# Attention weights turned by a transposing DMA: one row tile of each head leaves TensorE, and every engine's order is laid out anew

## The reference, cut to what matters

```python
for i in range(NUM_BLOCKS):                       # 4
    y = _cond_layer_norm(x, cond, s1_w[i], s1_b[i], b1_w[i], b1_b[i])
    y = _sparse_attention(y, src, dst, wq[i], bq[i], wk[i], bk[i], wv[i], bv[i], wo[i], bo[i])
    x = x + y
    y = _cond_layer_norm(x, cond, s2_w[i], s2_b[i], b2_w[i], b2_b[i])
    y = jax.nn.relu(y @ m_w1[i] + m_b1[i]) @ m_w2[i] + m_b2[i]
    x = x + y
```

## Time and profile before

| | |
|---|---|
| time, three runs | 1119.53 us median (1119.4 to 1120.54) |
| span of the profiled execution, first to last instruction | 1117.2 us; its own time is not listed apart |
| PE busy | 1066.1 us (95%) |
| DVE, ACT, POOL busy | 773.4, 577.6, 673.3 us |
| mean granted TensorE clock | 0.992 of full speed |

### The profile page before, as it was taken

How to read it: one execution, slowest core, us unless ns; L and a number is a source line. 1 busy time by engine, 2 the same in 40 slices (tenths; PEclk the granted TensorE clock), 3 DMA queues, 4 the chain that set the end, 5 groups by cost and what they waited for, 6 DMA issues and landing times.

```text
span 1117.2 us, 20722 instructions
## 1 busy us (share of the span) xinstructions
PE 1066.1 (95%) x6808; PEld 987.7 (88%) x6808; DVE 773.4 (69%) x1535; ACT 577.6 (52%) x1032; POOL 673.3 (60%) x923
## 2 busy tenths in 40 slices
...
GB/s 129 31 1 1 7 38 58 149 58 86 1 86 49 58 86 1 78 56 59 86 1 55 78 48 77 69 83 75 66 1 43 71 4 45 1 76 39 38 1 46
DMA packets 40963, 56.92 MB, mean 51 GB/s; under 512 B 14312, under 2 KB 14812, under 8 KB 40735
## 3 DMA queue, kind: packets, MB, share of 16 engines
...
## 4 chain that ended last, share of the span: by engine, by line
PE 79%; DVE 6%; POOL 5%; ACT 4%; issue 3%; DMA 2%; DVEq 0%; POOLq 0%; SPq 0%; PEldq 0%; ACTq 0%
PE ps L340 42%; PE ps L1768 8%; PE ps L362 8%; PE ps L786 5%; PE ps L2101 3%; PE ps L2028 3%; PE ps L2402 3%; POOL w_lo L380 2%; ACT away L737 1%; PE ps L2065 1%; PE ps L1259 1%; PE ps L1246 1%; PE ps L1742 1%; DMA w_raw<-L_gnn_wk 1%; PE ps L1220 1%
## 5 line engine op out<-in xcount | busy, mean ns | idle before, releaser
L380 POOL TENSOR_TENSOR w_lo<-w_raw,w_hi 128x512 fp32r<-128x512 f32 x152 | 204.8, 1348 | 12.7
L340 PE MATMUL ps<-yt_hi,w_hi 128*128 128x314 f32 (+2 forms) x640 | 201.8, 315 | 2.8 <-DVE yt_lo L2236 1.6
L340 PE MATMUL ps<-yt_hi,w_lo 128*128 128x314 f32 (+2 forms) x640 | 197.6, 309 | 0.0
L340 PE MATMUL ps<-yt_lo,w_hi 128*128 128x314 f32 (+2 forms) x640 | 197.3, 308 | 0.0
L459 POOL TENSOR_SCALAR prob<-prob,rinv 125x628 f32<-125x628 f32 x160 | 126.4, 792 | 105.2 <-DVE rinv L444 86.9
L403 ACT ACTIVATE pt_hi<-ps 125x625 fp32r<-125x625 f32 x160 | 109.2, 694 | 102.9 <-PE ps L362 101.7
L377 POOL TENSOR_SCALAR w_hi<-w_raw 128x512 fp32r<-128x512 f32 x152 | 97.7, 643 | 95.3 <-DMA w_raw<-L_gnn_wo 28.8
L340 PEld LDWEIGHTS ps<-yt_hi,w_hi 128*128 128x128 f32 x640 | 121.8, 190 | 5.9 <-issue 4.4
L340 PEld LDWEIGHTS ps<-yt_hi,w_lo 128*128 128x128 f32 x640 | 121.7, 190 | 0.0
L340 PEld LDWEIGHTS ps<-yt_lo,w_hi 128*128 128x128 f32 x640 | 121.5, 190 | 0.1
L786 PE MATMUL ps<-oh_s,oh_d 125*125 125x314 bf16 x800 | 111.4, 301 | 10.1 <-DVE oh_s L639 6.8
...
## 6 DMA issues: line engine op xcount, KB each, us to landing
...
```

The costliest lines, as they stand in the source:

```text
L340: ins = pe.matmul(out_ap, lhs(i, kk), rhs(j, kk), start=kk == 0 and n == 0, stop=kk == count - 1 and n == 2)
L380: pool.tensor_tensor(w[slot][1][:, kk, 0:cols], w_raw[slot][:, kk, 0:cols], w[slot][0][:, kk, 0:cols].bitcast(FP32), ALU.subtract).then_in ...
```

## The change

The first row tile of each of the middle stage's heads (`t0_0`, `t1_0`, `t2_0`, `t3_0`) is no longer turned by PE. ACT (`ex:`) copies the scaled tile as 16-bit halves into `planes`, low halves in five 128-wide blocks and high halves in five more; a transposing DMA on SP's queue (`turn:`) turns the ten blocks into `turned`, which lies over the tile's own place in `prob`; DVE (`jn:`) joins the halves into fp32 words over `planes`; `hi:` and `lo:` then read these words instead of PSUM. The score tile that reuses the place in `prob` (`sc:s1_0` for `t0_0`) waits for the join. All four lists are rewritten, SP's loads get a list `LOOP_SP`, the bias rows of the block share one buffer, and POOL clears `planes` once ahead of the stage. The last stage's lists do not change.

```diff
 LOOP_PE = """
-q0.0 q0.1 k1.0 k0.0 k0.1 k1.1 q1.0 s0_0 s0_1 s0_2 - q1.1 s0_3 q2.0 s0_4 t0_0 s1_0 - t0_1 q2.1 s1_1 t0_2 - k2.0
...
+q0.0 k0.0 q0.1 k0.1 q1.0 q1.1 s0_0 k1.0 s0_2 - s0_1 k1.1 - - s0_3 s0_4 - q2.0 - - s1_0 - t0_1 q2.1 t0_2 k2.0
+s1_1 - t0_3 k2.1 - s1_2 - t0_4 - - s1_3 - - pv0.0 - - s2_0 - t1_1 s1_4 pv0.1 - - - s2_1 k3.0 - - t1_2 - - t1_3
+k3.1 - - s2_2 - q3.0 - t1_4 s2_3 q3.1 - s2_4 - pv1.0 - - t2_1 - s3_0 pv1.1 s3_1 - - t2_2 - t2_3 s3_2 - s3_3 - -
+t2_4 - pv2.0 s3_4 - t3_1 pv2.1 - - t3_2 - - t3_3 - t3_4 - - pv3.0 pv3.1 - - o0.0 o0.1 - n2_0 o1.0 o1.1 - n2_1 -
...
+inv:s2_1 inv:s2_2 sc:s2_3 lo:t1_0 jn:t2_0 lo:t1_4 lo:q3 sc:s2_4 inv:s2_3 sc:s3_0 inv:s2_4 lo:t2_0 lo:t2_1
...
+row1:0 ws2 spo0 scale:s0_0 row1:1 row1:2 spo1 scale:s0_1 scale:s0_2 scale:s0_3 scale:s0_4 scale:s1_0 row1:3
...
+LOOP_SP = """
+turn:t0_0 turn:t1_0 load:k turn:t2_0 load:q row:1 turn:t3_0
+""".split()
...
+    def act_planes(act, u, buf):
+
+        halfwords = prob[:, u % RING_P, 0:N].bitcast(U16).rearrange("p (a b e) -> p e a b", a=TILES, e=2)
+        act.activation(planes[buf][0:R, :, 0:R].rearrange("p (e a) b -> p e a b", e=2), halfwords,
+                       ACT.Copy).then_inc(s_planes, 1)
+
+    def dve_joined(dve, u, buf, turned_count):
+
+        dve.wait_ge(s_turned, turned_count)
+        own(dve)
+        halfwords = joined[buf][:, 0:N].bitcast(U16).rearrange("p (a b e) -> p e a b", a=TILES, e=2)
+        dve.tensor_copy(halfwords, turned[u % RING_P][0:R, :, 0:R].rearrange("p (e a) b -> p e a b", e=2)).then_inc(s_joined, 1)
...
+                if kind == "turn":
+                    n = middle_turned.index(name)
+                    sp.wait_ge(s_planes, it * TURNS + n + 1)
+                    own(sp)
+                    sp.dma_start_transpose(turned[unit_of(name) % RING_P][:], planes[n % 2][:]).then_inc(s_turned, 16)
+                elif kind == "row":
+                    sp.wait_ge(s_xb, it * TILES + TILES)
+                    load_row(sp, 1, "L2_gnn_m_b2", it)
+                elif name == "q":
+                    jobs.wait_filled(sp, f"q{HEADS2 - 1}", at)
+                    load_w(sp, 1, "L2_gnn_m_w1", it, s_wl2)
+                else:
+                    jobs.wait_filled(sp, f"k{HEADS2 - 1}", at)
+                    load_w(sp, 2, "L2_gnn_m_w2", it, s_wl2)
...
+                if kind == "ex":
+                    u, n = unit_of(name), middle_turned.index(name)
+                    act.wait_ge(s_sc, it * UNITS + u + 1)
```

More of the change, by code:

```diff
@@ L42 @@
 RING_P = 5
+TURN = 640
 SMALL_RING = 8
@@ L144 @@
+f1.1 f2.1 - - f3.0 f3.1 - n1_0 n1_1 - p0.0 p0.1 - - p1.0 p1.1 p3.0 p3.1 - - p2.0 - a1_0 n1_3 p2.1 - a1_1 p4.0 -
+n1_2 p4.1 v0 a1_2 - v1 n1_4 - a1_3 - - v2 - a1_4 - - v3 - v4
 """.split()
 LOOP_DVE = """
-lo:k0 lo:q0 lo:k1 sc:s0_0 sc:s0_1 inv:s0_0 sc:s0_2 inv:s0_1 sc:s0_3 lo:q1 sc:s0_4 lo:t0_0 inv:s0_2 sc:s1_0
-lo:t0_1 inv:s0_3 sc:s1_1 inv:s0_4 lo:t0_2 inv:s1_0 lo:q2 sc:s1_2 lo:t0_3 lo:t0_4 sc:s1_3 inv:s1_1 lo:k2
-lo:t1_0 inv:s1_2 sc:s1_4 sc:s2_0 inv:s1_3 lo:pv0 lo:t1_1 sc:s2_1 inv:s1_4 lo:q3 lo:t1_2 inv:s2_0 inv:s2_1
@@ L149 @@
[L149 to L153, removed]
@@ L154 @@
-shift:n1_0 st:p2 res:p3 lo:a1_0 scl:n1_1 shift:n1_1 st:p3 res:p4 scl:n1_2 shift:n1_2 lo:a1_1 vb:v0 st:p4
-lo:a1_2 scl:n1_3 shift:n1_3 scl:n1_4 vb:v1 shift:n1_4 lo:a1_3 vl:v0 lo:a1_4 vl:v1 vb:v2 vl:v2 vb:v3 vl:v3
+lo:q0 lo:k0 sc:s0_0 lo:q1 inv:s0_0 sc:s0_1 sc:s0_2 inv:s0_1 lo:k1 sc:s0_3 sc:s0_4 jn:t0_0 inv:s0_2 inv:s0_3
+sc:s1_0 inv:s0_4 lo:q2 lo:t0_2 sc:s1_1 inv:s1_0 lo:t0_0 lo:t0_3 lo:t0_1 sc:s1_2 lo:k2 sc:s1_3 inv:s1_1 lo:t0_4
+jn:t1_0 sc:s1_4 inv:s1_2 inv:s1_3 sc:s2_0 inv:s1_4 sc:s2_1 lo:t1_1 lo:pv0 inv:s2_0 lo:t1_2 sc:s2_2 lo:t1_3 lo:k3
@@ new lines @@
+inv:s2_1 inv:s2_2 sc:s2_3 lo:t1_0 jn:t2_0 lo:t1_4 lo:q3 sc:s2_4 inv:s2_3 sc:s3_0 inv:s2_4 lo:t2_0 lo:t2_1
+inv:s3_0 lo:pv1 sc:s3_1 lo:t2_2 lo:t2_3 sc:s3_2 inv:s3_1 sc:s3_3 inv:s3_2 lo:t2_4 sc:s3_4 inv:s3_3 jn:t3_0
+inv:s3_4 lo:t3_1 lo:t3_0 lo:t3_2 lo:t3_3 lo:t3_4 lo:pv2 lo:pv3 res:o0 st:o0 scl:n2_0 shift:n2_0 res:o1 st:o1
+scl:n2_1 shift:n2_1 res:o2 st:o2 scl:n2_2 lo:a2_0 shift:n2_2 res:o3 st:o3 scl:n2_3 lo:a2_2 shift:n2_3 lo:a2_1
+res:o4 st:o4 scl:n2_4 shift:n2_4 lo:a2_3 lo:a2_4 lo:f1 lo:f0 lo:f2 lo:f3 res:p0 st:p0 scl:n1_0 res:p1 st:p1
@@ L158 @@
 LOOP_ACT = """
[L159 to L163, removed]
@@ L164 @@
-hi:a1_2 hi:a1_3 vh:v0 vh:v1 hi:a1_4 vh:v2 vh:v3 vh:v4
+hi:q0 hi:k0 hi:q1 exp:s0_0 ex:t0_0 exp:s0_1 hi:k1 exp:s0_2 exp:s0_3 exp:s0_4 hi:q2 hi:t0_2 hi:t0_0 exp:s1_0
+hi:t0_1 hi:t0_3 exp:s1_1 ex:t1_0 hi:k2 exp:s1_2 hi:t0_4 exp:s1_3 hi:t1_0 exp:s1_4 hi:t1_1 exp:s2_0 hi:pv0
+hi:t1_2 hi:t1_3 ex:t2_0 exp:s2_1 hi:k3 exp:s2_2 exp:s2_3 hi:q3 hi:t1_4 hi:t2_0 hi:t2_1 exp:s2_4 exp:s3_0 hi:pv1
+hi:t2_2 hi:t2_3 ex:t3_0 exp:s3_1 exp:s3_2 hi:t2_4 exp:s3_3 hi:t3_1 exp:s3_4 hi:t3_0 hi:t3_2 hi:t3_3 hi:pv2
+hi:t3_4 hi:pv3 hi:a2_0 hi:a2_2 hi:a2_1 hi:a2_3 hi:a2_4 relu:f1 relu:f0 hi:f1 relu:f2 hi:f0 hi:f2 relu:f3 hi:f3
@@ L165 @@
+hi:a1_0 hi:a1_1 vh:v0 hi:a1_2 hi:a1_3 hi:a1_4 vh:v1 vh:v2 vh:v3 vh:v4
 """.split()
 LOOP_POOL = """
[L167 to L170, removed]
```

181 lines of the change are left out of this document (127 added, 54 removed).

## The result

The changed kernel takes 1142.73 us (median of 4 runs, 1140.69 to 1144.11) against 1119.79 us for the one before (1119.4 to 1120.54) in the same comparison: ratio 1.0206, 95% interval 1.0192 to 1.022. It is 22.9 us slower; the forecast was 8.3 us slower.

A forecast was written before the change was run, and what follows sets the result against it. PE's work was taken to bound the kernel. Terms -8.8 - 4.0 + 11.0 + 5.2 + 1.6 + 3.3 = +8.3 on 1117.2 gave 1125.5, with 2.3 around it 1128 us; range 1113 to 1150.

The forecast's parts named there:

- The start of the block: PE waits in head 0 for `lo:k1`, then at `t0_1` and `t0_2`: +11.0 us over four blocks.
- lands 1.7 later: At each block's start, the last small load of modulation weights, `ws_raw`, lands 1.7 us after issue.
- the wait for k_lo: PE waits before `s1_0` for `lo:k1`: 3.0, 3.0, 0.5 and 0.5 us, 7.0 in all.
- the 4.0 that `t0_1` and `t0_2` were to add: Further PE waits in head 0: 0.7 and 0.4 us in block 1, 0.7 and 0.2 in blocks 0 and 3.
- the norm's wait: PE's 1.0 us wait per block before a norm's transposes goes: -4.0 us.
- the transposes: Five PE transposes less per head and block, 0.55 us per tile: -8.8 us.
- Head 2: Its transposing DMA queues behind a 1 MB load, so PE waits 1.3 us per block around `t2_1`: +5.2 us.
- The end of head 3: A join and two lo stand where one stood; pv3.0 waits about 1.0 in place of 0.6: +1.6 us.
- The seam: Between blocks, wk's split ends 1.1 us after the next block's start, at three seams: +3.3 us.
- The transfer: The transposing DMA of 320 KB on SP's queue takes 4 us, with 1.7 and 13.0 as ends.
- The slow rival: The transposing DMA takes 8 us in place of 4, all PE's: 57 us in all, 1185 us; chance 0.12.

The follow-up runs named there:

- the run with fillers: The changed kernel with 44 matmuls whose result nobody reads put ahead of `s1_0`, to keep the clock up: 1142.38 us.
- both edits on SP's queue: The changed kernel with the modulation weights' small loads issued early and head 2's transpose ahead of the 1 MB load waiting for k3: 1118.67 us.
- the best version: The changed kernel with early modulation weights, head 2's transpose ahead of the 1 MB load, and POOL's `spf0` behind `scale:s3_4`: 1115.49 us.
- the block's start mended: The changed kernel with the 16 small loads of modulation weights issued before SP's wait for the last v_lo and the wo load: 1122.47 us.
- the kernel with head 2's transpose alone: The changed kernel with only head 2's transpose moved ahead of the 1 MB load that waits for k3 on SP's queue: 1141.14 us.

## Why the prediction came out as it did

**Direction, place and chain: right.** Slower, by `ws2` ahead of the first scale; every step from the landing to `lo:k1` is in the traces with the lengths given: `ex` 1.25, exponential 0.81, `hi:k1` 0.77.

**The start of the block: mis-sized, 11.0 against 20.3.** The step that failed is "lands 1.7 later". I took it from the earlier trace rows, the landing of the tile `ws_raw`. The list of DMA issues of the kernel before shows what that number is:

```profile
ws_raw<-L_gnn_b_b SPq DMA_DIRECT2D x32, 2.0 KB
...
ws_raw<-one_row SPq DMA_DIRECT2D x4, 2.0 KB, 1.7
```

The 1.7 belongs to four rows of 2 KB loaded once, 39 to 41 us into the program, with only small loads ahead of them; the loads of the modulation weights have no landing time in the trace. Theirs, from the last issue to POOL's start, is 3.6, 3.4, 3.3 and 3.2 us in blocks 0 to 3. The Trainium skill (DMA: Bandwidth & Descriptors, Queues, rings and completion order) says that the count a transfer adds to a semaphore is a write that lands only after every earlier write of that DMA engine. Head 2's transfer agrees with it: issued 0.6 us behind the 1 MB load, it lands 1.2 us after that load (424.27 against 423.06 in block 1). For the last small load it gives no account by the megabyte: in blocks 0 to 2 wo had landed 1.5 to 1.9 us before that load was issued (376.72 against 378.19 in block 1). Why it takes twice the lone time is not shown. In block 0, besides, the wo load is issued 2.6 after the block's first matmul rather than 1.2, so the last issue comes 10.3 after it where I had 8.6. (In block 3 of the kernel before, whose first matmul is at 644.04, the last issue stood 9.0 after the start and not 8.8.) Together the weights are there 3.6, 1.7, 1.2 and 1.7 us later than I had them, 8.2 in all, and the wait for k_lo is 15.5 less 7.0, that is 8.5 larger. Of the 4.0 that `t0_1` and `t0_2` were to add little shows: a late `s1_0` gave POOL time. The other 4.8 of the 20.3 are near the 5.1 that three stretches at half clock take, which the sum did not have at all; the run with fillers got 1.5 of them back.

**Removed: the norm's wait right, the transposes mis-sized, 8.8 against some 2.** 80 matmuls less and 3.9 us of the norm's wait gone, as forecast. But PE's busy time in the four blocks is 559.82 us against 556.75, and 554.7 once the 5.1 of the half clock are taken out: 2.0 less, where five transposes per head and block were priced at 8.8. In the kernels with less waiting more of it comes through: 3.6 less with both edits on SP's queue, and 6.4 in the best version (1.7 of half clock taken out). Waits too short for the list may be part of this; no run shows it.

**Head 2: 5.2 forecast.** 2.8 as a wait in the trace; 3.8 in time with the block's start mended, 1.6, not clear of noise, without. Landing behind the load, 6.4, was seen as forecast (2.4 later than the 4 I had for one alone; 3.1 later than the 3.3 that one alone took).

**The end of head 3: +1.6 forecast, -2.4.** The wait of 0.6 a block for pt_lo ahead of `pv3.0` did not grow, it went: PE already waits for POOL's scales of head 3 just ahead of it. With these gone, in the best version, it is back with 2.8 over four blocks.

**The seam: 3.3 forecast, none.** wk was split 5.6 us after issue where I had 7.5, and the only wait for w_lo at a block's start is 0.8 in block 0. In the version with both SP edits the waits for w_lo are 3.1 us in the whole program, with wk landing after 6.6 beside the early small loads; whether it is that or the shorter blocks that brings the seam out is not shown. So the 3.3 was a term without a wait in the change.

**Not in my sum.** The half clock, 5.1. POOL's scales, mostly two waits of 0.4 per block in head 3, 3.8 in all; the edit against them was worth 3.2 us (1118.67 to 1115.49, from runs that lie in two groups). And block 3: the norms of the next block, which the new order puts between the MLP's halves, do not exist there, and PE waits 2.4 us for ht_lo and 0.9 for the last stage's input; before the change it waited 0.3 there. I read the lists for the loop only. That the missing norms are the reason is read from the lists; no run moves this one.

**The transfer: 4 forecast, 3.3 measured;** the join 1.4 against 0.88 alone and up to 1.64 beside POOL. The slow rival (8 us and more) is out.

**The whole.** By the traces of the two kernels, in the four blocks: waits for k_lo +15.5, for scales +3.8, for head 2's pt_lo +2.8, for ht_lo, xn and a norm in block 3 +3.5 less 0.3; the norm's wait -3.9, the one ahead of `pv3.0` -2.4; half clock +5.1; PE's own work -2.0. Together 22.1 of the 22.5 us that the blocks grew. This adds up what each cost where it stands; what mending one gives at the end is another number, as the runs show. The sum fell short of the 22.9 mainly by two terms, the landing (8.5) and the transposes' relief (6.8), and by the clock, which it did not have.

**What stays open.** Why so little of the transposes' time came off PE; why the last small load takes over 3 us; and what made the clock's stretches longer in the kernel with head 2's transpose alone.
